# Slot attention in a two-layer decoder: the order of one turn's steps written out by hand

## The reference, cut to what matters

```python
q, k = _rope(hs @ Wq.T), _rope(hs @ Wk.T)          # per head 256 x 128
v, g = hs @ Wv.T, hs @ Wg.T
s = clip(hs @ Ws1.T @ Ws2.T + bs2, -32, 32)         # per head 256 x 64
z = cumlogsumexp(s, axis=time); es = exp(s); enz = exp(-z)
A = where(tril, q @ k.T * DK ** -0.5, 0)
ok = enz * (A @ es)
qv = softmax(ok, axis=slots)
W2 = where(tril, (qv * enz) @ es.T, 0)
o = W2 @ v
o = o * rsqrt(mean(o * o) + eps) * g_norm_weight * silu(g)
x = x + o @ Wo.T
```

## Time and profile before

| | |
|---|---|
| median of 3 runs | 1915.8 us (1906.06 to 1917.16) |
| profiled execution | 1916.61 us, its span 1914.7 us, 51411 instructions |
| TensorE busy | 1700.4 us, 89% of the span |
| VectorE, ScalarE, GpSimd busy | 1268.8, 856.7, 560.2 us |
| slot attention, first to last `qk` rotation | 25.7 to 507.7 us |
| share of the chain of waits: TensorE, VectorE, ScalarE | 64%, 20%, 6% |
| mean granted TensorE clock over the span | 0.947 |

### The profile page before, as it was taken

The page is one execution under the profiler, slowest core; times in us unless marked ns, Lnnn a source line. Parts: engine busy times, 40 slices in busy tenths (PEclk is TensorE's granted clock), DMA queues, the critical chain, the costliest instruction groups (busy, mean ns, idle before and its releaser), DMA issues.

```text
span 1914.7 us, 51411 instructions
## 1 busy us (share of the span) xinstructions
PE 1700.4 (89%) x21686; PEld 1186.2 (62%) x21686; DVE 1268.8 (66%) x2850; ACT 856.7 (45%) x1404; POOL 560.2 (29%) x951
## 2 busy tenths in 40 slices
PE   5999999999977888899899989997888889899988
PEld 4888888888855346555466545664554445566557
DVE  7766667675656877778888553444356687789844
ACT  3333333433333164556656722441232465567652
POOL 5544434433314140230501022441111222322230
PEclk9999999999988799999999989998897999999999
DMA  3000000110004636334263374655602134554100
GB/s 114 31 12 12 23 34 2 34 57 12 17 3 97 115 57 147 59 93 97 45 143 68 67 264 149 216 179 119 127 1 48 36 74 92 115 110 80 33 2 23
DMA packets 91857, 143.94 MB, mean 75 GB/s; under 512 B 14870, under 2 KB 60123, under 8 KB 91628
## 3 DMA queue, kind: packets, MB, share of 16 engines
q1 hardware_dynamic: 87228, 127.79, 28.6%
q10 hardware_dynamic: 2528, 7.74, 1.2%
q0 software_dynamic: 1872, 5.13, 0.7%
HBM read 109.68 MB, written 32.03 MB: 74 GB/s over the span
## 4 chain that ended last, share of the span: by engine, by line
PE 64%; DVE 20%; ACT 6%; issue 6%; POOL 2%; DMA 1%; SPq 1%; DVEq 0%; another core or an unknown queue 0%; ACTq 0%; POOLq 0%
PE bank L1045 17%; PE bank L1253 6%; PE bank L1998 5%; DVE shared L1326 3%; PE bank L1884 3%; PE bank L777 3%; PE bank L1886 3%; PE bank L1885 3%; PE bank L2017 3%; DVE xa_part_max L1326 3%; PE bank L2460 2%; PE bank L2445 2%; ACT xa_e L1287 2%; PE bank L742 2%; DVE da_neg L2579 1%
## 5 line engine op out<-in xcount | busy, mean ns | idle before, releaser
L1326 DVE TENSOR_REDUCE xa_part_max<-bank 128x1 f32<-128x448 f32 (+1 forms) x512 | 266.2, 567 | 23.5 <-PE bank L1045 21.3
L1287 ACT ACTIVATE xa_e<-bank 128x1024 f32<-128x1024 f32 (+1 forms) x208 | 212.2, 1024 | 131.3 <-PE bank L1045 129.6
L1287 ACT ACTIVATE ca_e<-bank 128x1024 f32<-128x1024 f32 (+2 forms) x208 | 197.2, 958 | 81.8 <-PE bank L1045 79.6
L1326 DVE TENSOR_REDUCE shared<-bank 128x1 f32<-128x400 f32 (+1 forms) x384 | 205.6, 569 | 33.9 <-PE bank L1045 30.2
L1045 PE MATMUL bank<-xa_kst,xa_qst 122*32 122x448 bf16 (+1 forms) x2048 | 183.9, 354 | 16.0 <-DVE xa_part_max L1326 8.1
L1253 PE MATMUL bank<-xa_e,xa_vaug 128*17 128x256 f32 (+1 forms) x1664 | 135.4, 383 | 7.6 <-issue 3.5
L1045 PE MATMUL bank<-xa_qst,xa_kst 128*32 128x256 bf16 (+1 forms) x3264 | 136.5, 276 | 5.1 <-issue 3.2
L1253 PE MATMUL bank<-ca_e,ca_vaug 128*17 128x256 f32 (+2 forms) x1664 | 128.8, 377 | 10.0 <-issue 6.2
L981 POOL TENSOR_TENSOR gsa_qk<-gsa_qk,gsa_rot 128x512 f32<-128x512 f32 x64 | 81.9, 1279 | 164.7 <-DVE gsa_rot L897 164.7
L1045 PE MATMUL bank<-xa_wkv,shared 128*32 128x256 f32 (+1 forms) x1632 | 114.3, 393 | 9.7 <-SPq L281 3.2
L1045 PEld LDWEIGHTS bank<-xa_qst,xa_kst 128*32 128x32 bf16 (+1 forms) x3264 | 94.0, 97 | 36.3 <-issue 8.1
(11 more groups left out here) (408 smaller groups left out, 4232.9 us busy)
## 6 DMA issues: line engine op xcount, KB each, us to landing
xa_kst<-xa_k_parts SPq DMA_DIRECT2D x96, 200.1 KB, 5.0
ca_kst<-ca_k_parts SPq DMA_DIRECT2D x96, 200.1 KB, 5.1
xa_k_parts<-xa_parts SPq DMA_DIRECT2D x24, 400.2 KB, 4.3
ca_k_parts<-moe_ctx_parts SPq DMA_DIRECT2D x8, 1200.8 KB
moe_gu<-in_expert_gate_up SPq DMA_DIRECT2D x8, 1024.0 KB
shared<-in_ctxT_split ACTq DMA_DIRECT2D x4, 1601.0 KB, 9.7
moe_ctxT<-in_ctxT SPq DMA_DIRECT2D x8, 800.5 KB, 8.1
ca_cv<-in_ctx SPq DMA_DIRECT2D x4, 1536.0 KB
```

Of the source, the lines that this page charges most:

```text
L1287: e.activation(self.e[m % 3][0:rows, :, first:T], banks[m % 2][0:rows].rearrange("p a (h t) -> p (a h) t", t=T)[:, :, first:T], ACT.Exp, s ...
L1326: e.tensor_reduce(top, work[:, 0:hi - lo], AX.X, ALU.max).then_inc(*reduced(t, *step))
```

## The change

For turns 0 to 14, `turn(m)` yields the same steps as the three woven lists, each once, in an order that is written out. In turns 15 to 18 the order is as before. The early steps of the next stage are woven into turns 12 and 14 as before.

```diff
--- before.py
+++ after.py
@@ -554,6 +554,34 @@
                 if n // B == GROUPS - 1 and n % B < B - 1:
                     yield from list(norm_steps(1, n % B))[:-TB]
 
+            def turn(m):
+                g, r = divmod(m, B)
+                s, p = G4 * m, 2 * (m - 2)
+                parts = [[], []]
+                for part, at_, key in ((0, 2, "q"), (1, 2, "k"), (0, 3, "v")):
+                    if r == at_ and g + 1 < GROUPS:
+                        parts[part].append(("w_split", g + 1, key))
+                if r == 0 and g < GROUPS:
+                    if g == 0:
+                        parts[0].append(("w_split", 0, "v"))
+                    parts[0].append(("w_split", g, "g"))
+                if r == 1 and g < GROUPS:
+                    parts[0].append(("wo_scale", g))
+                if r == 3 and g and g + 1 < GROUPS:
+                    parts[1].append(("wo_load", g + 1))
+                units = {"qk": G4, "ok": G4, "a": G4, "z": 2, "w2": 2, "gate": 2, "o": 2}
+                for step in (
+                    ("qk", s), ("v", m - 1, 0), ("ok", s - G4), ("u", m), ("sm_exp", m - 2), ("v", m - 1, 1),
+                    ("ok", s - 3), ("rr", m - 3), ("scale", m - 3, 0), ("a", s - 2), ("qk", s + 1), ("a", s - 1),
+                    *parts[0], ("es", m), ("gate", p), ("z", p), ("z", p + 1), ("ok", s - 2),
+                    ("scale", m - 3, 1), ("ot", m - 3, 0), ("qk", s + 2), ("gate", p + 1), ("w2", p, 0), ("w2", p, 1),
+                    ("ok", s - 1), ("ot", m - 3, 1), ("cs", m), ("a", s), ("w2", p + 1, 0), ("o", p),
+                    ("w2", p + 1, 1), ("qk", s + 3), ("wo", m - 3, 0), ("et", m), ("sm_max", m - 1), ("a", s + 1),
+                    *parts[1], ("wo", m - 3, 1), ("o", p + 1)):
+                    kind, n = step[:2]
+                    if kind in ("w_split", "wo_scale", "wo_load") or 0 <= n // units.get(kind, 1) < (B if kind == "u" else GSA_UNITS):
+                        yield step
+
             def xa_early(m):
 
                 if m == GSA_UNITS - 4:
@@ -595,7 +623,10 @@
             yield from normed_rows(2)
             yield from normed_rows(3)
             for m in range(GSA_UNITS + 3):
-                main = list(weave(list(weave(list(scores(m)), list(ahead(m)))), list(behind(m)), lead=8))
+                if m < GSA_UNITS - 1:
+                    main = list(turn(m))
+                else:
+                    main = list(weave(list(weave(list(scores(m)), list(ahead(m)))), list(behind(m)), lead=8))
                 if m < GSA_UNITS + 2:
                     yield from weave(main, list(xa_early(m)))
                 else:
```

## The result

The changed kernel takes 1855.4 us (median of 4 runs, 1849.2 to 1864.1) against 1914.8 (4 runs) beside it: ratio 0.9695, 95% interval 0.9648 to 0.9742. Two later comparisons gave 0.9741 (0.9705 to 0.9778; 1859.4 against 1911.8 us) and, with more runs, 0.9726 (0.9698 to 0.9753; 1869.1 against 1920.9 us). The forecast was 1884, range 1866 to 1900: the direction and the mechanism held, the size did not. The profiled execution took 1852.66 us.

What follows compares the result with a forecast made beforehand. TensorE, busy 89% of the span, was taken as the bound. Waits 29.7 plus clock 13.0, less costs of 4.8, 1.6 and 3.6, gave 32.7 us off 1916.6: 1884 us, range 1866 to 1900.

Steps and rivals of the forecast that it cites:

- what is there to win: Turns 1 to 14: TensorE's idle time, waits adding to 29.7 us, and 26.5 us at the lower clock.
- Step 5: Turns 3, 7, 11: GpSimd's split of k holds VectorE's subtraction, `rr` is late, `ok` waits for the selection; 4.8 us cost.
- Step 6: Weight splits of q, v and g standing mid-turn ahead of scale 1: 0 to 1 us each, 1.6 us cost booked.
- Step 7: Turn 15, old order again, `cs` close behind `es`: 1.9 us wait and up to 1.7 of clock, 3.6 us cost.
- Steps 1 and 2: TensorE's waits go: `cs` for the exponential 10.0 us, `qk` for its bank 8.0, `w2` for `z` 7.8, `scale` 2.0, `w2T` 1.9.
- Step 3: Slot attention's low clock follows TensorE's waits and goes with them: 13.0 us gained, at least nothing.
- A clock that falls all the same: Rival, chance 0.10: low clock stays in slot attention without the waits, price 13.0 us, so 1897 us, or about 1894.
- Hold-ups in every turn: Rival, chance 0.12: `rr` ends later, `ok` waits some 1.6 us in each of 14 turns, 22.4 us; 1909 us.
- ScalarE's copy behind `o`: Rival "slower", chance 0.05: ScalarE's copy of `w2` p+1 waits for a late `o` p and blocks its queue; 1937 us.

## Why the prediction was wrong in size

**The first failed step is "what is there to win".** The 29.7 us of the earlier trace rows were taken for the whole price of the waits, and 1874 for a bound. The idle column starts at the modelled end of the product before. For the wait of the earlier trace rows, `a`'s last product is this one:

```profile
353.21 0.38 PE L717 MATMUL bank<-gsa_qk 128*128 128x128 f32 x2
```

From its start to the next, 355.53, it is 2.32 us; undisturbed the same step is 0.22 (314.39 to 314.61). So 2.10 us are lost where the column says 1.94, and by the kernel with `z` put back the products behind a wait lose a little more. The term measured: 29.3 of idle and 6.9 beyond it, 36.2, not 29.7. At the 0.30 of that kernel the 26 waits give 7.8 for the 6.9.

**The second is the costs that I booked against the gain**, 10.0 us in steps 5, 6 and 7. None of them came, and they are the larger part of the error inside slot attention.

**Steps 1 and 2** held: none of the named waits is left from turn 2 on, and the span between producer and consumer that was checked is as added up (`es` to `cs` 8.3 forecast, 9.0 less `es` 0.9 = 8.1 measured). The eight steps that I counted between `qk`+2 and `qk`+3 are ten; nothing hangs on it. **Step 3** held: no low clock where no waits are; 27.3 us of it before cost 12.0, by the 0.44 above, for 13.0. That idle is the cause is supported by all sixteen profiles together, with a reservation. Up to the end of turn 14 a low stretch stood at none of 82 waits of 0.9 to 1.4 us, at 24 of 37 of 1.9 to 2.0 us, and at all twelve of 3.2 to 3.4 us. What decides in the middle case is not shown.

**Step 5**: the margin was right to 0.2 us, and the hold-ups of `rr` came as booked. The 4.8 us for turns 3, 7 and 11 did not, for two reasons. I had VectorE's subtraction behind the start of GpSimd's split, and it was 0.28 us ahead; which starts first decides. And I had put VectorE's idle time at nothing: with the split moved ahead of it, 1.45 us of idle took in the hold-up in two turns of three. By the Trainium skill (SBUF — State Buffer, Who interferes with whom), issue order decides who blocks; the trace agrees, 0.69 us with VectorE 0.28 ahead (the split took 2.65 then, for 2.36) and 2.41 with GpSimd 0.49 ahead. **Step 6**, 1.6 us: nothing came. **Step 7**, 3.6 us: wrong by reading. In turn 15's own list `qk` and `ok` stand between `es` and `cs`; I had carried the list of turn 6 over. No wait of `cs` came there.

The sum with what was measured: 36.2 + 12.0 = 48.2 by the end of turn 14, and 2.0 by the seam, 50 us, where I had 29.7 + 13.0 - 10.0 = 32.7. Of the 17.5 between them, 10.0 are costs that were booked and did not come, 6.5 the hidden part of the waits (36.2 for 29.7), and 2.0 the seam, less 1.0 of clock. That corrects the forecast to 1866, the lower end of the range, and no further. The rest of the first measurement's 59 us lies behind slot attention, where I had no term at all: 13.9 us between the two profiled executions, in stages that the change leaves alone. By the medians, less the gain up to the first square root in the profiles, it was 9.2 us in the first comparison and 3.5 and 2.1 in the two later ones. No run shows that it belongs to the change, so that the first median fell as far as 1855 stays in that part unexplained, and may be chance.

**The rivals.** A clock that falls all the same: rejected, 1.00 throughout. Hold-ups in every turn: `rr` was held, but `ok` waited in no turn of the changed kernel, and in one with the split of k moved. ScalarE's copy behind `o`: that chain never showed as a wait of TensorE in the changed kernel.

## What to carry to other kernels

Price a wait of TensorE from start to start, against the same step undisturbed, and not by the idle column; then add the clock that follows it. In a list that several engines walk, look for the step whose input crosses two other engines and count what stands between it and its producer: one such step at the wrong place cost 5.0 us a turn, of which about 3.2 showed as idle. A walk through the new list is worth making to tell where margins are thin, but a cost should be booked only where the margin is clearly negative, and the idle time of the engines in between has to be walked too.

## What the runs showed of the hardware

A wait of the same length does not always lower the clock: the four waits of 1.93 us for the exponential had a low stretch behind each of them in the kernel before, and behind two of them where only the split of g was moved. Three waits of 1.94 us for a rotation had one behind each before, and none in the kernel with `cs` moved. And the same stage, cross attention with identical instructions, took 592 to 612 us in six profiles of two kernels, at a mean granted clock of 0.93 to 0.96. A chain of tiny VectorE operations is held up by GpSimd as well as a large one: 0.75 and 1.20 us for 0.10 and 0.17.
